# Cross-attention and LoRA mixture kernel: pair scores in eight matmuls of 512 columns, and the exponentials' exchange issued by two engines

## The reference

```python
def _L0_xattn_ref(hidden_states, memory_tokens, memory_mask):
    scores = jnp.einsum('bsd,bmd->bsm', hidden_states, memory_tokens) * scale
    scores = jnp.where(memory_mask[:, None, :], scores, neg_inf)
    attn = jax.nn.softmax(scores, axis=-1)
    readout = jnp.einsum('bsm,bmd->bsd', attn, memory_tokens)
    ...
def _L0_ffn_ref(x, weight, lora_A, lora_B, router_w):
    base = jnp.einsum('btd,od->bto', x, weight)
    logits = jnp.einsum('btd,ed->bte', x, router_w)
    ... # softmax, the best 2 of 8 experts, their gates w_dense
    Ax = jnp.einsum('nd,erd->ner', x_flat, lora_A)
    expert_out = jnp.einsum('ner,ne,eor->no', Ax, w_dense, lora_B) * SCALING
    return base + expert_out
x = x + _L0_xattn_ref(_layernorm(x), ctx_2048, mask)
x = x + _L0_ffn_ref(_layernorm(x), weight, lora_A, lora_B, router_w)
```

## Time and profile before

| what | value |
|---|---|
| median of 3 runs | 984.8 us (983.56 to 985.69) |
| the profiled execution | 983.32 us, its span 981.2 us |
| granted TensorE clock, mean | 0.998 |
| busy: TensorE, VectorE, ScalarE, GpSimd | 99%, 87%, 48%, 15% |
| the chain that ended last | TensorE 89%, VectorE 5%, DMA 2%, the rest 1% or less each |

### The profile page before, as it was taken

The page is one execution under the profiler, slowest core; times in us unless marked ns, Lnnn a source line. Parts: engine busy times, 40 slices in busy tenths (PEclk is TensorE's granted clock), DMA queues, the critical chain, the costliest instruction groups (busy, mean ns, idle before and its releaser), DMA issues.

```text
span 981.2 us, 18824 instructions
## 1 busy us (share of the span) xinstructions
PE 973.7 (99%) x6081; PEld 961.7 (98%) x6081; DVE 850.0 (87%) x2201; ACT 474.5 (48%) x930; POOL 144.2 (15%) x278
## 2 busy tenths in 40 slices
PE   8999999999999999999999999999999999999998
PEld 7999999999999999999999999999999999999998
DVE  6988988889888998889988899888998889888774
ACT  6755544545444455445455445454454454453420
POOL 3311111111111111111111111111111111111110
PEclk9999999999999999999999999999999999999999
DMA  9646565655566555565555755556655566554522
GB/s 323 216 131 166 157 172 159 179 132 153 165 175 181 164 124 160 165 193 157 154 137 156 203 138 169 140 140 196 162 161 163 124 191 168 160 159 127 122 67 76
DMA packets 156095, 156.61 MB, mean 160 GB/s; under 512 B 93968, under 2 KB 128912, under 8 KB 156048
## 3 DMA queue, kind: packets, MB, share of 16 engines
q1 hardware_dynamic: 155184, 154.63, 56.8%
q10 hardware_dynamic: 864, 1.45, 0.4%
HBM read 78.74 MB, written 33.55 MB: 114 GB/s over the span
## 4 chain that ended last, share of the span: by engine, by line
PE 89%; DVE 5%; DMA 2%; issue 1%; SPq 1%; ACT 1%; POOL 0%; ACTq 0%; DVEq 0%; POOLq 0%
PE base_ps L1100 26%; PE base_ps L1101 25%; PE base_ps L1102 25%; PE ro_ps L1174 3%; PE ro_ps L1175 3%; PE s_ps L1129 2%; PE s_ps L1127 2%; PE base_ps L1206 1%; DMA xq<-xn 1%; DVE stats L898 1%; DMA xT_raw<-in_xT 1%; DVE x2T L914 1%; DVE w_raw L892 1%; SPq L379 1%; ACT xn L607 0%
## 5 line engine op out<-in xcount | busy, mean ns | idle before, releaser
L1100 PE MATMUL base_ps<-w_hi,xT_hi 128*128 128x392 f32 x1512 | 495.5, 328 | 0.0
L1101 PE MATMUL base_ps<-w_lo,xT_hi 128*128 128x392 f32 x1512 | 494.4, 327 | 0.0
L1102 PE MATMUL base_ps<-w_hi,xT_lo 128*128 128x392 f32 x1512 | 494.4, 327 | 0.0
L1100 PEld LDWEIGHTS base_ps<-w_hi,xT_hi 128*128 128x128 f32 x1512 | 285.8, 189 | 1.7
L1101 PEld LDWEIGHTS base_ps<-w_lo,xT_hi 128*128 128x128 f32 x1512 | 285.8, 189 | 1.6
L1102 PEld LDWEIGHTS base_ps<-w_hi,xT_lo 128*128 128x128 f32 x1512 | 285.8, 189 | 0.0
L914 DVE STREAM_TRANSPOSE x2T<-xq 128x512 f32<-128x512 f32 x122 | 166.1, 1465 | 19.7 <-DMA xq<-xn 19.4
L492 POOL TENSOR_TENSOR rstd<-var_eps,neg_half 128x1 f32<-128x1 f32 x64 | 61.8, 966 | 504.1 <-DVE var_eps L905 504.1
L613 ACT CAST xT_hi<-x2T 128x512 fp32r<-128x512 f32 x122 | 69.5, 617 | 106.2 <-DVE x2T L914 106.2
L588 ACT CAST eT<-w_raw 128x128 fp32r<-128x128 f32 x59 | 17.6, 299 | 151.7 <-DMA w_raw<-w_raw 151.7
L921 DVE TENSOR_TENSOR xT_lo<-x2T,xT_hi 128x512 fp32r<-128x512 f32 x122 | 78.3, 682 | 0.0
(11 more groups left out here) (132 smaller groups left out, 1391.5 us busy)
## 6 DMA issues: line engine op xcount, KB each, us to landing
xT_raw<-in_xT SPq DMA_DIRECT2D x62, 512.0 KB, 5.3
xq<-xn SPq DMA_DIRECT2D x244, 128.0 KB, 3.5
w_raw<-in_x SPq DMA_DIRECT2D x32, 512.0 KB, 3.5
out<-x_first SPq DMA_DIRECT2D x32, 512.0 KB, 2.7
out<-w_raw SPq DMA_DIRECT2D x31, 512.0 KB, 2.8
x_first<-in_x SPq DMA_DIRECT2D x30, 512.0 KB, 3.6
h<-w_raw SPq DMA_DIRECT2D x248, 16.0 KB, 2.0
w_raw<-w_raw SPq DMA_DIRECT2D x236, 16.0 KB, 2.6
```

The lines of the kernel that those rows point to most:

```text
L1100: pe.matmul(out_, a_hi, w_h, start=start, stop=False, skip_group_check=again)
L1101: pe.matmul(out_, a_hi, w_l, start=False, stop=False, skip_group_check=again)
L1102: return pe.matmul(out_, a_lo, w_h, start=False, stop=stop, skip_group_check=again)
```

## The change

The pair scores become eight matmuls of 512 columns: the moving operand takes the high and the low part of x side by side, so that the products with the high part add up in the left half of `s_ps` and those with the low part in the right half. ScalarE copies the right half to SBUF (`s_low`), VectorE adds the two halves to `s_sum` and transposes that. The exchange of the exponentials is issued in halves: pieces 0 and 1 by SyncE as before, pieces 2 and 3 by ScalarE, between the mean and the squares of the first norm. The same sums are computed, in another order.

```diff
+        s_sum = w_raw[0][:, C - 4, 0:T2]
+        s_low = w_raw[0][:, C - 5, 0:T2]
...
# SyncE
                 sp.wait_ge(eq_done, count(tile, 1, 1 - 5))
-                for i in range(Q):
+                for i in range(Q // 2):
                     sp.dma_start(e_raw[:, i * QP:(i + 1) * QP], eq[i * QP:(i + 1) * QP, :]).then_inc(e_loaded, 16)
...
# ScalarE
+            def e_exchange(tile):
+                act.wait_ge(eq_done, count(tile, 1, 1 - 5))
+                for i in range(Q // 2, Q):
+                    act.dma_start(e_raw[:, i * QP:(i + 1) * QP], eq[i * QP:(i + 1) * QP, :]).then_inc(e_loaded, 16)
...
+            def s_low_copy(tile):
+                act.wait_ge(sT_done, pairs(tile, 1, 1))
+                act.copy(s_low, s_ps[:, T2:2 * T2]).then_inc(s_low_copied, 1)
...
                     norm1_mean(after(tile, 3))
+                if exists(nxt2) and not turned_on_pe(nxt2, 5):
+                    e_exchange(nxt2)
+                if exists(after(tile, 3)):
                     norm1_squares(after(tile, 3))
                 gate_exp(tile)
...
                     eT_copy(nxt2)
+                if j % 2 == 1 and exists(after(tile, 3)) and not turned_on_pe(after(tile, 3), 6):
+                    s_low_copy(after(tile, 3))
                 if exists(nxt):
                     x2T_high(nxt)
...
# VectorE
             def s_transposes(tile):
-                dve.wait_ge(sT_done, pairs(tile, 1, 1))
+                dve.wait_ge(s_low_copied, pairs(tile, 1, 1 - 3))
+                dve.tensor_tensor(s_sum, s_ps[:, 0:T2], s_low, ALU.add).then_inc(s_sum_done, 1)
+                dve.wait_ge(s_sum_done, pairs(tile, 1, 1 - 3))
                 dve.transpose(sq.rearrange("p (j k c) -> p k j c", k=2, c=QP),
-                              s_ps[:, 0:T2].rearrange("p (j c k) -> p k j c", k=2, c=QP)).then_inc(sq_done, 1)
+                              s_sum.rearrange("p (j c k) -> p k j c", k=2, c=QP)).then_inc(sq_done, 1)
...
# TensorE
                 for c in range(C):
-                    pe.matmul(s_ps[:, 0:T2], ctxT[:, c, :], xT_hi[:, :, c, :].rearrange("p t n -> p n t"),
-                              start=(c == 0), stop=False)
-                    mm = pe.matmul(s_ps[:, 0:T2], ctxT[:, c, :], xT_lo[:, :, c, :].rearrange("p t n -> p n t"),
-                                   start=False, stop=(c == C - 1))
+                    mm = pe.matmul(s_ps[:, :], ctxT[:, c, :], xT_parts[:, :, :, c, :].rearrange("p k t n -> p k n t"),
+                                   start=(c == 0), stop=(c == C - 1))
                 mm.then_inc(sT_done, 1)
```

More of the change, by code:

```diff
@@ L321, in xattn_lora_moe_kernel @@
         e_loaded = sem("e_loaded")
+        s_low_copied = sem("s_low_copied")
+        s_sum_done = sem("s_sum_done")
         sq_done = sem("sq_done")
```

## The result

| | before | changed |
|---|---|---|
| median | 984.78 us (983.56 to 985.69) | 1009.18 us (1008.03 to 1009.91) |
| span of the profiled execution | 981.2 us | 1008.1 us |

The ratio is 1.025, with a 95% interval of 1.0237 to 1.0262. The change costs 24.4 us where 12 were forecast and up to 23 were in the range. The direction was right, the size was not.

A forecast was written before the change was run, and what follows sets the result against it. TensorE was taken to bound the kernel, with no room. The terms -2.0 - 1.6 + 2 + 10.5 + 3.8 gave +12.7 us on 983.3, so 996.0; forecast 997 us, range 985 to 1008.

The forecast's parts named there:

- The pair matmuls: TensorE's pair scores: eight wide matmuls take 1.72 us instead of 1.79, a gain of 2.0 us over 29 pairs.
- e lands some 0.4 us earlier in spite of Part 2: Exchange of the exponentials: SyncE's last issue ends at 511.63 instead of 512.04, so e lands 0.4 us earlier.
- Part 2: Adding the score halves: ScalarE's copy, VectorE's add and hand-overs make the pair transpose 0.86 us later.
- +2 - 1.6 us: Even steps' hT_lo waits cost 2 us; the five readout waits for eT go, at most 1.6 us gained.
- j = 4: Step that prepares a batch: eT late for the readout, a 1.5 us wait seven times, 10.5 us.
- The place of the even steps' wait: TensorE before LoRA in 22 even steps: waits 0.1 us each for hT_lo, 2 us.
- The late transposes: VectorE's pair transpose comes 0.86 us later; the transpose from SBUF was taken to last as long as from PSUM.
- ScalarE's issues: Two issues between mean and squares, 0.635 us each; in even steps VectorE is 0.78 us late at gate_den.
- j = 3: Step before the batch-preparing one: hT_lo late where xq lands late, about 0.95 us four times, 3.8 us.
- Rival B: Still dearer: issues start only after the mean, or e's pieces hold up xq's; 1003 to 1012 us, chance 0.20.
- DMAs issued by two engines: Quoted skill rule: several issuers' DMAs interleave on the same engines, and only issuing time is saved.

The follow-up runs named there:

- e5: The changed kernel with half of every xq piece left out (64 KB instead of 128 KB each); 992.33 us in one execution.
- e1: The kernel before with only the scores' part of the change, all four exchange pieces issued by SyncE; 1000.07 us, ratio 1.017.
- e2: The kernel before with only the exchange's part of the change, sixteen pair matmuls of 256 columns kept; 990.45 us, ratio 1.0076.
- e10: As e2, but in steps j = 4 SyncE issues all four pieces and ScalarE none; 984.63 us, ratio 1.0007.
- e12: As e8, with the next batch's two token loads moved from the end of j = 1 to the ends of j = 0 and j = 2; 984.22 us.
- e8: As e1, with the eight wide pair matmuls moved ahead of the second half of base group 1; 990.14 us, ratio 1.0059.
- e4: The changed kernel with ScalarE's two issues moved behind gate_exp; 1008.09 us, ratio 1.0247.
- e6: As e1, but without copy and add: VectorE transposes the left half of the wide matmuls' bank at once; 984.04 us, ratio 1.0004.
- e9: The changed kernel with the eight wide pair matmuls moved ahead of the second half of base group 1; 1004.46 us, ratio 1.0211.
- e13: The changed kernel with SyncE's store of the output tile moved behind the exchange of h; 1011.14 us, ratio 1.0272.

## Why the prediction was wrong

- **The pair matmuls.** The eight were forecast at 1.72 us and take 1.72; -2.0 us was forecast, and regular odd steps gained 0.06 us each, 1.7 us in all. Right, though a few irregular steps (the longest 16.2 us) give it back, so that j = 1, 5 and 7 stand at +0.8.
- **The step that failed: "e lands some 0.4 us earlier in spite of Part 2".** It took the last issue's end for what sets e's landing. That held before, but by 0.1 us only: with two issues fewer, what is ahead of e on the DMA engines, xq, sets it. The last issue ended 1.3 us sooner behind xn, and eT came 0.1 us sooner (7.64 for 7.74 us); e5, with half of xq's bytes, gave 0.9 to 1.2 us. So the even steps pay for xn's lateness of 0.75 us, less the 0.4 us that eT had in hand there (it ended at 513.68, the readout began at 514.08). Instead of +2 - 1.6 us they cost 12 us. On the scale of the sums by step, where +12.7 was forecast and +27.6 measured, this is 11.6 us of the 14.9 that are missing; the rest lies at j = 4 and in the odd steps.
- **The place of the even steps' wait.** hT_lo before LoRA was forecast. It is eT before the readout. The margin of eT (0.4 us) was put down at j = 4 and not for the even step. By itself this would not have changed the forecast, as e was taken to come earlier there; it would have shown what hangs on that step.
- **The late transposes.** 0.86 us was forecast. xn starts some 0.75 us later against LoRA; the add takes 0.46, the copy 0.37, and the transpose from SBUF 0.51 where the one from PSUM took 0.46 in the mean. The means by line, of before in the first row and of the changed kernel in the others:

```profile
L873 DVE STREAM_TRANSPOSE w_raw<-s_ps 128x256 f32<-128x256 f32 x29 | 13.4, 463 | 7.4 <-PE s_ps L1129 7.4
...
L893 DVE STREAM_TRANSPOSE w_raw<-w_raw 128x256 f32<-128x256 f32 x29 | 14.8, 510 | 1.0
L891 DVE TENSOR_TENSOR w_raw<-s_ps,w_raw 128x256 f32<-128x256 f32 x29 | 13.4, 464 | 0.5 <-ACT w_raw L631 0.5
L631 ACT COPY w_raw<-s_ps 128x256 f32<-128x256 f32 x29 | 10.8, 372 | 39.0 <-PE s_ps L1147 38.9
```

- **ScalarE's issues.** 0.635 us apiece behind the e transpose was right (median 0.62), and gate_den came late as forecast (432.96 with LoRA at 425.96, that is 7.00 us behind it, where it was 6.28).
- **j = 4.** +10.5 us was forecast, by the late transposes and ScalarE's issues together, and +11.9 measured: 4.6 us in e1 and 7.0 in e2. Right, and the issues' share is shown by e2 and e10. The changed kernel's readout there, TensorE's timeline:

```profile
467.32 0.48 PE L1192 MATMUL ro_ps<-ctx_hi,eT 128*128 128x512 f32 x1 [1.53 <-ACT eT L597]
```

- **j = 3.** +3.8 us, measured +2.9. Right in size; it is spread over six batches and not four. It hangs on xq's lateness: in the scores' part, with the tokens' loads moved, e12 has -0.5 us there, where e8 has +2.6.
- **Rival B.** 1009.18 us lies in its interval, but by neither of its mechanisms, so that would have been luck. The first issue started before the mean was through, and xq was not held up by e's pieces (VectorE's waits for it are 19.0 us after 19.4, its median to landing 3.6 us after 3.5). It is e that xq holds up.
- **DMAs issued by two engines.** The Trainium skill ("DMA: Bandwidth & Descriptors", Issuing engines are not separate DMA queues) says that issuing from two engines saves only the issuing time. The trace agrees that pieces of two issuers travel among each other: ScalarE's packets move while xq's last ones do (4.4 to 5.7 us behind xn). The prediction quoted it, made it the ground of rival B, and then counted the issuing time as a gain in landing. The runs go further: with xq's bytes ahead, of 1.3 us of issuing time saved 0.1 us arrived, for the landing took 3.6 and 3.2 us behind the issue instead of 2.6. The changed kernel's issues, median to landing in the last column (the two queues share a semaphore, and its landings are credited to the issues in their order, so the two rows are to be read together):

```profile
w_raw<-w_raw ACTq DMA_DIRECT2D x118, 16.0 KB, 3.6
w_raw<-w_raw SPq DMA_DIRECT2D x118, 16.0 KB, 3.2
```

What stays open: why eT starts 1.4 us behind the last of e's recorded packets in the changed kernel (they end 6.2 us behind xn), where it is 0.4 us in before and in e5, so how xq's bytes hold up a landing whose own packets are through; and why the tokens' loads hurt j = 3 less in some kernels (e4, e10) than in others.

## What to carry to other kernels

Before a transfer's issue is made cheaper, see how far behind the issue's end it lands, and how far behind the producer of the bytes that travel ahead of it: two limits can lie as close as 0.1 us, as here, and then taking one away gains no more than that. An experiment that moves only the bytes ahead (e5) tells them apart. Write down the margin at every place where the bound engine can wait, in every kind of step, and ask of each number that keeps such a margin safe what it rests on. A delay behind a wait that is fixed to the bound engine goes into what follows: leaving the delayed work out (e6) took the cost of the even steps away, and so did moving its source earlier on that engine (e8), in the scores' part alone; with both parts together (e9) it took away less than 5 us.

## What the runs showed of the hardware

- A DMA issue on ScalarE's queue starts while an arithmetic instruction still runs (430.07 within the mean that ends at 430.33), and the next arithmetic instruction waits for both issues (1.17 us).
- An issue takes 0.55 to 1.89 us there (median 0.62 of 118, two over 0.9). The two steps with the long ones were 0.5 and 0.7 us longer than the others, as this one in the changed kernel, a step j = 2 that lasts 15.12 us. SyncE's four issues of xq, 2.54 us elsewhere, take 3.77 us there and end at the same moment, 186.86, so both queues were held up. ScalarE's issues are not needed for it: in e1, without them, this step lasts 15.67 us. What holds the queues up is open.

```profile
183.09 3.77 SPq L383 DMA_DIRECT2D xq<-xn  x4
...
185.02 1.84 ACTq L592 DMA_DIRECT2D w_raw<-w_raw  x1
186.98 1.15 ACT L563 ACTIVATE x2T<-w_raw,neg_mean 128x1024 f32<-128x1024 f32 x1 [2.31 <-issue]
```

- eT started 1.3 us behind the end of the last 16 KB issue when that came 2.6 us behind the issue of xq's 512 KB (before, e1), or closer behind 256 KB (e5). With the 512 KB issued 1.3 to 1.6 us ahead it was 2.2 to 2.7 us (changed, e2, e13).
- A block transpose of 128x256 takes 0.46 us from PSUM and 0.51 us from SBUF in the mean, both with a stride of two elements.
